# New weights and durations for the planner that orders a decoder layer's instructions

## The reference

```
x = x + attention(layernorm(x))        # 16 heads of 16, causal, ALiBi, softmax, biases on q, k, v and output
x = x + cross(layernorm(x), ctx, mask) # one head of 256, own sequence of ctx only, keys = values = ctx
x = x + ffn(layernorm(x))              # 256 -> 1024 -> 256, tanh GELU, biases
```

## Time and profile before

| | before |
|---|---|
| runs | 131.90, 132.09, 132.27 us |
| median | 132.09 us |
| profiled execution | 132.44 us |
| its span, first to last instruction | 130.6 us |
| TensorE busy, products | 116.4 us (89%) |
| VectorE (DVE) | 103.5 us (79%) |
| ScalarE (ACT) | 88.7 us (68%) |
| GpSimd (POOL) | 81.5 us (62%) |
| mean granted TensorE clock | 1.000 |

### The profile page before, as it was taken

One profiled execution on the slowest core, in us unless ns is written; L12 is line 12 of the kernel. 1 busy time (PEld: TensorE's weight loads), 2 busy tenths in 40 slices (PEclk: granted clock), 3 DMA queues, 4 the chain that ended last, 5 costly groups with the idle time before them and its releaser, 6 DMA issues.

```text
span 130.6 us, 3224 instructions
## 1 busy us (share of the span) xinstructions
PE 116.4 (89%) x1072; PEld 87.8 (67%) x1072; DVE 103.5 (79%) x227; ACT 88.7 (68%) x190; POOL 81.5 (62%) x144
## 2 busy tenths in 40 slices
PE   0997999698999899999989996979989599999990
PEld 0996447265534786677767684758878389999980
DVE  5678794799999999899999998778743985685632
ACT  1224679776999987977757875687957877754520
POOL 7685700153999976638038898787764567894330
PEclk9999999999999999999999999999999999999999
DMA  4799906999500000000000000000000200020202
GB/s 119 206 364 374 354 16 260 365 356 373 119 3 3 0 5 0 5 0 0 5 0 0 0 8 0 0 0 3 5 0 0 79 1 5 0 80 0 85 3 80
DMA packets 8879, 10.69 MB, mean 82 GB/s; under 512 B 1664, under 2 KB 7936, under 8 KB 8736
## 3 DMA queue, kind: packets, MB, share of 16 engines
q1 hardware_dynamic: 7776, 9.64, 22.1%
q10 hardware_dynamic: 1088, 0.86, 2.0%
HBM read 9.45 MB, written 1.05 MB: 80 GB/s over the span
## 4 chain that ended last, share of the span: by engine, by line
PE 29%; DVE 26%; POOL 18%; issue 18%; ACT 6%; DVEq 1%; POOLq 0%; ACTq 0%
POOL h_hi L630 6%; PE bank L1028 5%; PE bank L1176 5%; PE bank L1160 5%; DVE s_sb L857 5%; POOL rstd L603 5%; DVE s_max L862 4%; POOL var_eps L599 3%; PE bank L1040 3%; POOL x_sb L634 2%; DVE stats L810 2%; PE bank L1067 2%; PE bank L1059 2%; PE bank L1015 2%; POOL s_sb L641 2%
## 5 line engine op out<-in xcount | busy, mean ns | idle before, releaser
L641 POOL TENSOR_TENSOR s_sb<-s_sb,s_max 128x512 f32<-128x512 f32 x16 | 18.6, 1165 | 18.4 <-DVE s_max L862 18.2
L982 DVE TENSOR_TENSOR h_lo<-h_sb,h_hi 128x256 fp32r<-128x256 f32 x32 | 15.1, 485 | 7.6 <-POOL h_hi L630 7.5
L1160 PE MATMUL bank<-xn_T,w_up_q 128*128 128x256 f16 x128 | 19.4, 274 | 1.4 <-ACT h_sb L778 1.4
L778 ACT ACTIVATE h_sb<-bank,bias_cols 128x256 f32<-128x256 f32 x32 | 15.0, 472 | 7.7 <-PE bank L1160 5.9
L1176 PE MATMUL bank<-w_down_q,h_hi 128*128 128x256 f32 x64 | 19.2, 324 | 0.2 <-DVE h_lo L982 0.2
L630 POOL CAST h_hi<-h_sb 128x256 fp32r<-128x256 f32 x32 | 13.9, 440 | 8.0 <-ACT h_sb L778 7.6
L660 ACT ACTIVATE xn<-x_sb,shift,rstd 128x256 f32<-128x256 f32 x20 | 12.0, 599 | 7.7 <-POOL shift L607 3.2
L1176 PE MATMUL bank<-w_down_q,h_lo 128*128 128x256 f32 x64 | 16.4, 280 | 0.0
L603 POOL TENSOR_TENSOR rstd<-var_eps,minus_half 128x1 f32<-128x1 f32 x24 | 14.9, 622 | 2.0
L1028 PE MATMUL bank<-xn_T,w_T 128*128 128x512 f32 x32 | 14.7, 601 | 0.8 <-ACT xn_T L672 0.8
L599 POOL TENSOR_SCALAR var_eps<-mean_var 128x1 f32<-128x1 f32 x24 | 7.3, 304 | 10.7 <-DVE mean_var L811 9.5
(11 more groups left out here) (89 smaller groups left out, 265.5 us busy)
## 6 DMA issues: line engine op xcount, KB each, us to landing
raw_T<-in_W_up_T_dram SPq DMA_DIRECT2D x1, 1024.0 KB, 9.2
raw<-in_W_up_dram SPq DMA_DIRECT2D x1, 1024.0 KB, 11.5
raw_T<-in_W_down_T_dram SPq DMA_DIRECT2D x1, 1024.0 KB, 5.0
raw<-in_W_down_dram SPq DMA_DIRECT2D x1, 1024.0 KB, 7.8
ctx_T<-in_ctx_by_feature_dram SPq DMA_DIRECT2D x1, 1024.0 KB, 10.1
ctx_sb<-in_ctx_dram SPq DMA_DIRECT2D x1, 1024.0 KB, 13.8
out_dram<-x_sb SPq DMA_DIRECT2D x8, 128.0 KB, 1.7
x_sb<-in_x_dram SPq DMA_DIRECT2D x4, 128.0 KB, 3.1
```

Source lines behind the costliest of these rows:

```text
L641: pool.tensor_tensor(tile, tile, s_max[:, u % S_RING, :].unsqueeze(2).broadcast_to([P, HC, S]), ALU.subtract).then_inc(centred, 1)
L778: act.activation(h_sb[:, i % GELU_RING, :], bank[up_bank(i)][:, 0:GN], ACT.Gelu_apprx_tanh, bias=bias_cols[:, BUP + f:BUP + f + 1], scale= ...
L982: dve.tensor_tensor(h_lo[:, i % H_RING, :], h_sb[:, i % GELU_RING, :], h_hi[:, i % H_RING, :].bitcast(F32), ALU.subtract).then_inc(split_r ...
L1160: last = pe.matmul(dst[:, 0:GN], w_up_q[:, c, f * P:(f + 1) * P], xn_T16[:, g * GT:(g + 1) * GT, at16:at16 + P], start=(k == 0), stop=(k = ...
```

## The change

The structure of `stages()` and `schedule()` is the same. Durations in the table change for `rstd`, `add_bo`, `v2_zero2`, `k_flat`, `x_fill`, `q_divide` and the ACT table load. All urgencies, drifts and patiences are replaced. No instruction is added, removed or altered; their order on each engine's queue follows from the new numbers.

```diff
-        add("rstd", (n, t), "pool", 1.18 if norm_on_act(n, t) else 0.85, [("stats", (n, t))])
+        add("rstd", (n, t), "pool", 1.22 if norm_on_act(n, t) else 0.87, [("stats", (n, t))])
...
-    add("v2_zero2", (), "dve", 1.6)
+    add("v2_zero2", (), "dve", 2.3)
-            add("add_bo", (t,), "pool", 0.7, [("norm", (LN1, t)), ("load_row_biases", ())])
+            add("add_bo", (t,), "pool", 1.1, [("norm", (LN1, t)), ("load_row_biases", ())])
-            add("k_flat", (h, c), "act", 0.5, [("k", (h, c))] + (keys[0, c] if h else []))
+            add("k_flat", (h, c), "act", 0.54, [("k", (h, c))] + (keys[0, c] if h else []))
...
-    add("x_fill", (), "pool", 1.4)
+    add("x_fill", (), "pool", 1.6)
...
-        for name, us in (("q_divide", 1.13), ("q_exponent", 0.6), ("q_step", 0.6), ("q_add", 1.13), ("q_round", 1.13),
+        for name, us in (("q_divide", 1.85), ("q_exponent", 0.6), ("q_step", 0.6), ("q_add", 1.13), ("q_round", 1.13),
...
-ACT_TABLE_US = 1.3
+ACT_TABLE_US = 1.4
...
-    "quant": 142, "scores": 84, "attn_turn": 84, "k": 68, "q": 51, "q_inverse": 51, "normalise": 50,
-    "scale_T": 43, "final": 40, "warm": 39, "load_mask": 37, "rows_copy": 37, "amax": 36, "centre": 35,
-    "reload": 35, "q_clip": 31, "binade": 31, "low": 30, "v2_zero": 29, "up": 25, "valid": 25, "load_ctx": 24,
-    "pv": 23, "load_up": 21, "x_mask": 21, "v_even": 21, "load_v": 19, "max": 18, "spread": 18, "add_down": 17,
-    "x1": 16, "v_own": 16, "q_out": 15, "k_rest": 14, "load_rows": 14, "x_max": 13, "x_table": 11,
-    "load_qk": 11, "v_move": 11, "v_copy": 9, "v_spread": 9, "turn": 8, "x_prob_copy": 7, "load_vo": 6, "x2": 5,
-    "q_cut": 4, "x_prob_T": 4, "round": 3, "rstd": 3, "load_blocks": 2, "load_alibi": 2, "prob_copy": -5,
-    "attn_copy": -7, "prob_T": -7, "turn_copy": -8, "x_scale": -8, "qk_bias": -16, "split": -16,
-    "q_exponent": -17, "load_biases": -18, "x_read": -18, "x_fill": -22, "load_x": -22, "v_odd": -23,
-    "load_o": -24, "k_flat": -25, "stats": -25, "gelu": -26, "add_bo": -27, "spread_copy": -27, "v2_zero2": -28,
-    "exp": -29, "load_row_biases": -30, "q_divide": -30, "store": -30, "v": -31, "down": -36,
-    "load_weights": -40, "q_round": -41, "k_copy": -41, "scale_copy": -42, "q_step": -43, "add": -48,
-    "norm": -50, "x_scores": -57, "q_copy": -59, "x_exp": -73, "q_add": -101, "out_proj": -101,
+    "quant": 142, "prob_copy": 115, "spread": 100, "attn_copy": 71, "x_max": 65, "split": 60, "load_mask": 55,
+    "rows_copy": 55, "x_prob_T": 51, "centre": 49, "max": 47, "store": 46, "scale_copy": 46, "up": 45,
+    "k_rest": 45, "round": 45, "spread_copy": 41, "scale_T": 40, "load_row_biases": 39, "k": 36, "v2_zero": 32,
+    "rstd": 31, "add_down": 28, "v_even": 27, "turn_copy": 27, "x_read": 27, "amax": 25, "pv": 25, "q_out": 22,
+    "load_up": 21, "x_mask": 21, "q": 20, "load_ctx": 18, "v_own": 16, "normalise": 14, "valid": 14,
+    "attn_turn": 13, "q_add": 13, "x1": 11, "v_move": 11, "load_weights": 10, "q_copy": 10, "v_copy": 9,
+    "v_spread": 9, "turn": 8, "v2_zero2": 8, "load_vo": 6, "norm": 1, "load_biases": -3, "exp": -6,
+    "q_divide": -6, "k_copy": -6, "out_proj": -6, "v_odd": -8, "q_clip": -9, "load_o": -10, "k_flat": -10,
+    "low": -11, "qk_bias": -11, "warm": -13, "gelu": -14, "load_alibi": -15, "down": -15, "q_step": -16,
+    "binade": -17, "load_blocks": -17, "add_bo": -18, "x_table": -21, "x_scores": -21, "x_scale": -24,
+    "q_exponent": -26, "load_rows": -27, "x2": -27, "stats": -30, "q_round": -30, "q_inverse": -31,
+    "load_v": -31, "final": -32, "load_x": -34, "x_prob_copy": -35, "scores": -39, "x_fill": -39, "reload": -41,
+    "x_exp": -46, "q_cut": -53, "load_qk": -61, "add": -63, "v": -69, "prob_T": -110,
-    "q_exponent": 68.8, "v2_zero": 48.0, "q_inverse": 32.0, "reload": 24.0, "q_copy": 22.4, "q_step": 19.2,
-    "k_flat": 16.0, "v_copy": 12.0, "q_clip": 8.0, "x_scores": 7.2, "store": 7.2, "x_mask": 6.4, "stats": 5.0,
-    "v_spread": 3.2, "q_round": 3.2, "spread": 2.4, "k": 2.4, "attn_turn": 2.4, "prob_copy": 2.0,
-    "spread_copy": 0.8, "add_bo": 0.8, "x_exp": 0.8, "final": 0.8, "pv": 0.6, "split": 0.2, "norm": -0.8,
-    "exp": -1.2, "gelu": -1.6, "round": -1.8, "up": -2.0, "rstd": -2.1, "add": -2.4, "prob_T": -3.0,
-    "turn_copy": -3.7, "q": -5.6, "out_proj": -6.0, "centre": -6.8, "x_max": -8.4, "normalise": -8.4,
-    "x_prob_copy": -8.8, "max": -8.8, "x_scale": -9.2, "scores": -11.6, "add_down": -14.8, "scale_T": -20.2,
-    "amax": -20.8, "v_even": -23.2, "k_copy": -24.0, "v_move": -24.0, "warm": -37.3, "v_odd": -70.4,
-    "scale_copy": -79.9, "q_add": -169.6, "q_divide": -171.2,
+    "v2_zero": 48.0, "q_cut": 27.2, "q_clip": 24.0, "q_round": 24.0, "q_add": 24.0, "x_prob_copy": 23.6,
+    "q_inverse": 16.0, "store": 14.0, "q": 13.6, "v_copy": 12.0, "normalise": 9.6, "v_odd": 9.6, "x_mask": 6.4,
+    "turn": 4.3, "k": 4.0, "x_scale": 4.0, "round": 3.5, "reload": 3.2, "v_spread": 3.2, "x_scores": 2.8,
+    "x1": 2.8, "up": 2.1, "attn_turn": 2.0, "low": 2.0, "prob_T": 1.6, "q_divide": 1.6, "stats": 1.3,
+    "k_flat": 0.8, "final": 0.8, "split": 0.7, "norm": 0.6, "down": -0.2, "add": -0.4, "turn_copy": -0.7,
+    "exp": -1.0, "spread": -2.0, "rstd": -2.1, "q_copy": -2.4, "pv": -2.4, "prob_copy": -3.0, "centre": -3.0,
+    "attn_copy": -4.0, "spread_copy": -5.2, "add_down": -6.0, "k_copy": -7.2, "x_max": -8.0, "load_x": -8.0,
+    "x_read": -8.8, "x2": -8.8, "x_exp": -10.0, "max": -11.4, "out_proj": -14.4, "v_even": -23.2,
+    "v_move": -24.0, "amax": -26.4, "q_exponent": -27.2, "binade": -40.0, "q_step": -160.0,
+    "scale_copy": -200.0,
-    "pool": 0.54, "act": 0.04, "dve": 0.0, "pe": 0.0,
+    "pool": 1.2, "dve": 0.08, "act": 0.0, "pe": 0.0,
```

## The result

The changed kernel takes 133.66 us in the median of 11 runs (132.97 to 134.33); the kernel before, run beside it, takes 132.09 (11 runs, 131.36 to 132.86). The ratio is 1.0116, with a 95% interval of 1.0083 to 1.0149: slower by 1.2%. Forecast was 131.1. The time lies inside the range, but the direction is wrong. The profiled execution took 133.08 us, its span 131.3. In the experiments a few executions fell in a slower state of the chip, and the medians and ratios given leave them out.

The account below looks back on a forecast made before the run. TensorE was taken as the bound, with only its idle time open to change. Terms 0 - 0.3 - 1.2 + 0.5 + 0 = -1.0 us gave 131.1 us; own range 130.2 to 131.7, wide range 129.2 to 133.8.

Parts of the forecast that it names:

- TensorE bounds the kernel: Whole kernel: TensorE has the least idle time from 20 us on; an order can only remove or add idle time.
- The first 20 us: Start of the kernel: seldom more than one stage ready, so 0 us, from 0 to +0.7.
- 20 to 60 us: A `centre` on POOL should no longer stand behind three additions: -0.3 us, from -0.8 to +0.8.
- The down weight: Its quantisation on DVE runs nearly together and ends earlier, removing TensorE's first stall: -1.2 us, from -1.9 to +2.1.
- TensorE's queue: 44 to 104 us: late tiles' probabilities turned later, which can delay the last softmax: +0.5 us, from -0.4 to +1.5.
- the stretch on POOL: POOL operations lengthened beside DVE's down weight operations: 3.74 us excess on the chain that releases ACT.
- what is late next: After ACT's waits for `norm`: TensorE regains 1.23 us; the 0.71 behind the table load stays; 1.2 taken.
- The FFN's rhythm: Last stretch: 22 steps of 0.92 us, already without a gap: 0 us, from -0.2 to +0.3.
- The rival on the other side: 70 to 82 us: DVE's train shuts POOL out during the last softmax: +1.7 us, 133.8; slower 0.33.
- The third rival: Second GELU table exchange costs TensorE nothing, another 0.92 + 0.40 us given back: 129.8 us; chance 0.10.
- The other signs: Right: first-GELU gap under 0.5 us, rhythm from near 103.4. Wrong: rhythm starting after 104.4 or not 0.92 us.

Follow-up runs that it names:

- One swap: Old head, new middle, old tail, with gelu(1) put ahead of norm(1,5) on ACT: 131.18 us, 0.9957 of the kernel before; middle segment 53.19 against 53.83 without the swap.

## Why the prediction was wrong

- **TensorE bounds the kernel, and only idle time can change: right.** Busy time 116.2 against 116.4 us.
- **The first 20 us, 0: right** as far as order goes; the 0.88 us that the traces differ there is not the change's.
- **In all, forecast -1.0, measured +1.55.** The 2.55 us between them are 1.04 in the head, 0.35 in the middle, and 1.16 behind it.
- **20 to 60 us, -0.3 (from -0.8 to +0.8): measured +0.74** in the head. Within the bounds, with the wrong sign and the wrong stage. I priced `centre` behind additions; with the additions gone it waits for DVE's `max`, and TensorE for neither. I never listed what the new weights do to ACT's copies: `v_odd`, from -23 with a drift of -70.4 to -8 with +9.6, and `v_even` are in the diff, and 0.47 us hangs on the places of two copies in ACT's queue.
- **The down weight, -1.2, and TensorE's queue, +0.5: together -0.7 forecast, -0.35 measured,** and -0.15 with the rest of the order as before. This comes near by luck: the gain isn't where it was forecast. Up to `x_read`(6), behind the quantisation and the first GELUs, the new order had lost 0.12 us, and the whole gain was made at the second exchange of tables, which the forecast left alone. The table load did come earlier (1.66 us from `scores`(4)), but the stretch on POOL, 3.74 us, was taken as gone and is 3.72: it only fell on others. Part of it is now on the `rstd` of a `norm` that stands ahead of `attn_copy`(6), hence the 1.52 us. And the step "what is late next" stopped at the first GELU; the second, behind a waiting `norm`, decides, since `up` has two banks. One swap shows its price, 0.64 us. Four turns were priced at about twice the 0.44 us of two; their rows have 0.60 to 0.66.
- **The FFN's rhythm, 0 (from -0.2 to +0.3): the step that failed.** Measured +0.65 in the rhythm and +0.51 at its end, 1.16 of the 1.55. I took "already without a gap" for "can't be disturbed", and priced none of POOL's stages inside it, though `add_down`'s drift (-14.8 to -6.0) is in the diff. What they cost is shown: 0.51 for `add_down`(7) beside the last `split`, 0.32 for `add_down`(5), and the late `rstd` of tiles 6 and 7, for whose `norm` and turns ACT and TensorE wait. Which of the new numbers puts these stages there, the durations, the weights or the patience, no run separates.
- **The rival on the other side gave nearly the time, 133.8, and half of its mechanism.** The last exp starts at 78.90, which looks short of the 79.0 from which it was to decide. Counted from `k`(0,0), though, it is 1.45 us later than before (66.93 against 65.48), 0.74 of it from the head. What delays the last `centre` (1.04 us at 77.79, not lengthened) is the `rstd` ahead of it, lengthened by 0.51 + 0.98 beside the step and the addition on DVE. But the price of 1.7 us wasn't paid there: up to `x_read`(6) 0.12 was lost, and there is no fifth table load. That the time fits is luck.
- **The third rival's place gave something.** The second exchange of tables costs 0.85 us instead of 1.32, where it priced 1.32 as gone.
- **The other signs.** The first GELUs' idle time on TensorE is 0.74 us, not under 0.5. The stretch of `up` and `down` starts at 103.87, not near 103.4; from `k`(0,0) that is 0.39 later than before, so the sign of being wrong, a start after 104.4, was met. And the rhythm has steps of 1.42 us, which I had named as such a sign too; but steps of 1.14 and 1.24 us are in the kernel before as well, so "22 steps of 0.92" was a misreading of its last ones.

## What to carry to other kernels

Where one engine is full, price the stages that the other engines do inside its steady loop first: a few of them, crowded or put beside the last step, cost more here (1.16 us) than the whole stretch ahead of the loop gave back (0.35). An operation lengthened by its neighbour isn't shortened by moving the neighbour unless nothing takes its place, and an engine's queue in order makes the awaited copy as late as the one ahead of it: list, for each TensorE wait, what stands before its releaser. Compare executions by segments between the same stages, since these repeat to 0.02 us where the whole doesn't, and cut until the gain lies in a stretch short enough to name its cause: the middle looked like the forecast's success until one more cut put its gain elsewhere.

## What the runs showed of the hardware

The time until the first k product differs from one execution to the next by up to 1.5 us (11.64 to 13.18 over the fourteen traces), with the same instructions in the same order on TensorE. Of the changed kernel and of the one with `add_down`(7) moved, at the same six products of constants:

```profile
6.96 0.88 PE L1009 MATMUL bank<-const 128*128 128x128 f32 x6
```

```profile
7.01 1.49 PE L1023 MATMUL bank<-const 128*128 128x128 f32 x6
```

These start 0.05 us apart and take 0.61 us more or less. Four of the fourteen traces have them at 0.83 to 0.88, ten at 1.31 to 1.49 (the kernel before at 1.49). What tells them apart is the moment at which TensorE's clock rises. In each trace the products of constants start 0.21 us apart at first and 0.11 us apart from some moment on, and the record of the full clock (2.4 GHz, of the two levels) begins at that moment: at 7.06 in the changed kernel, at 8.88 in the kernel before, at 6.39 to 7.06 in the four traces, and at 7.89 to 9.53 in the ten. Up to then TensorE is at work from 3.3 to 3.6 us on, mostly on these products. The fourteen starts of `k`(0,0) follow these moments: 11.64 for the earliest and 13.18 for the latest, 1.54 us for 3.14, about half, as it should be where the slower level has half the pace. The 1.82 us between the kernel before and the changed one make 0.9 in this way, and the first column has 0.88. It isn't the order's doing: kernels with the same beginning have it at 6.39 and at 9.53. The mean granted clock of the page doesn't show it (1.000 in the kernel before, 0.995 in the changed one): there is no record before the rise, and the lower mean comes from a fall to half at 129.94, when TensorE is done. A profiled span alone can hide a loss of 0.9 us, as here.

In two neighbouring rows of the changed kernel the one of DVE and POOL that starts second is lengthened, once each. The rounding of 128x2048 on DVE takes 1.68 us at 78.24 where the earlier trace rows has 1.22: it starts beside a `centre` that ends at 78.83, and ends 1.09 us behind that, at 79.92. POOL's epsilon addition starts at 78.92 beside this rounding and takes 1.08 where 0.22 is plain: it ends at 80.00, 0.08 behind the rounding.
